# A norm, a projection, a convolution and the rates of a state-space branch moved into the steps of the layers that follow; a causal mask and the first fetches moved too

## The reference

```python
xn = layernorm(x)
x = x + L0_attn(xn) + L0_ffn(xn)          # causal, 16 heads; 8 experts, top 2
xn = layernorm(x)
x = x + L1_attn(xn) + L1_ffn(xn)

def L1_attn(x):                            # the branch
    xn = (x - mu) * rsqrt(var + EPS) * gamma + beta
    xin, z = split(xn @ W_in.T + b_in)     # 256 channels each
    xc = silu(causal_conv1d(xin, conv_w, taps=15) + conv_b)
    dt_low, Bm, Cm = split(xc @ W_x.T)     # 8, 16, 16
    delta = softplus(dt_low @ W_dt.T + b_dt)
    h_t = h_(t-1) * exp(delta_t * A) + delta_t * B_t * xc_t   # 16 states
    y = sum_n(h * C) + xc * D_param
    return x + (y * silu(z)) @ W_out.T + b_out

def L1_ffn(x):                             # the layers
    for i in range(6):
        x = attn_layer(shift_tokens(x), ...) + x   # 16 heads of 64, window 32, rotary, l2norm
        x = ffn_layer(shift_tokens(x), ...) + x    # layer norm, 341 gated units, gelu
    return x
```

## Time and profile before

| | us |
|---|---|
| median of 3 runs | 3053.31 |
| lowest, highest | 3052.78, 3054.47 |
| the profiled execution | 3048.94 |
| its span, first to last instruction | 3047.1 |
| attention of block 0 and opening, to the drain | 1208.9 |
| prologue of the layers, to the first instruction of step 0 | 62.1 |
| the rest, steps and tail | 1776.1 |

### The profile page before, as it was taken

One profiled execution on the slowest core, in us unless ns is written; L12 is line 12 of the kernel. 1 busy time (PEld: TensorE's weight loads), 2 busy tenths in 40 slices (PEclk: granted clock), 3 DMA queues, 4 the chain that ended last, 5 costly groups with the idle time before them and its releaser, 6 DMA issues.

```text
span 3047.1 us, 98549 instructions
## 1 busy us (share of the span) xinstructions
PE 2865.7 (94%) x41200; PEld 1881.2 (62%) x41200; DVE 2261.1 (74%) x3547; ACT 1754.5 (58%) x2617; POOL 1672.8 (55%) x1471
## 2 busy tenths in 40 slices
PE   6999999999999998898999999999999999999996
PEld 5555556555666656465666666666666666666664
DVE  2666565584677776877888888887888878888773
ACT  2544555545666665455666566665666666665553
POOL 0000001100466665476888788887788868887652
PEclk7999999999999999999999999999999999999998
DMA  2000000000011111134334334432433343333222
GB/s 92 1 1 1 1 1 1 1 1 10 15 46 46 45 46 40 46 105 125 89 87 117 85 80 117 92 86 76 111 96 89 80 109 93 80 88 81 68 68 56
DMA packets 181658, 188.24 MB, mean 62 GB/s; under 512 B 77598, under 2 KB 128548, under 8 KB 179684
## 3 DMA queue, kind: packets, MB, share of 16 engines
q1 hardware_dynamic: 181220, 181.94, 23.8%
HBM read 60.99 MB, written 6.03 MB: 22 GB/s over the span
## 4 chain that ended last, share of the span: by engine, by line
PE 78%; DVE 8%; issue 5%; ACT 3%; SPq 3%; POOL 2%; DMA 1%; DVEq 0%; ACTq 0%; POOLq 0%
PE ps L1318 16%; PE ps L581 13%; PE ps L1326 5%; PE ps L1411 5%; PE ps L1369 5%; PE ps L1333 5%; PE ps L616 4%; PE ps L594 4%; PE ps L1378 2%; PE ps L528 2%; PE ps L1432 2%; PE ps L1425 2%; PE ps L599 2%; DVE nmx L685 2%; PE ps L1359 2%
## 5 line engine op out<-in xcount | busy, mean ns | idle before, releaser
L1318 PE MATMUL ps<-wqkv,xcT 128*128 128x512 f32 x1152 | 558.2, 607 | 53.6 <-issue 31.9
L581 PE MATMUL ps<-xnT,qp 128*128 128x512 f32 (+3 forms) x1280 | 527.5, 543 | 15.5 <-ACT prob L803 14.6
L1934 POOL TENSOR_TENSOR ra<-ra,rb 128x1024 f32<-128x1024 f32 x192 | 452.1, 2360 | 160.7 <-DVE rb L1814 159.9
L811 ACT ACTIVATE probT<-ps 128x512 f32<-128x512 f32 (+3 forms) x384 | 207.7, 541 | 385.8 <-PE ps L594 385.8
L803 ACT ACTIVATE prob<-ps,ebias,unit 128x1024 f32<-128x1024 f32 (+7 forms) x384 | 360.3, 954 | 113.8 <-DVE ebias L692 55.0
L581 PEld LDWEIGHTS ps<-xnT,qp 128*128 128x128 f32 x1280 | 232.2, 191 | 272.2 <-issue 227.7
L1953 POOL TENSOR_TENSOR ra<-ra,rn 128x1024 f32<-128x1024 f32 x192 | 361.6, 1904 | 7.5
L1318 PEld LDWEIGHTS ps<-wqkv,xcT 128*128 128x128 f32 x1152 | 196.0, 190 | 222.1 <-issue 208.3
L685 DVE TENSOR_REDUCE nmx<-ps 128x1 f32<-128x1024 f32 (+7 forms) x256 | 245.7, 986 | 109.7 <-PE ps L581 95.3
L1589 ACT ACTIVATE sq<-ps 128x1024 f32<-128x1024 f32 x192 | 195.2, 1017 | 95.8 <-PE ps L1318 95.4
L1812 DVE TENSOR_TENSOR ra<-ps,tab 128x1024 f32<-128x1024 f32 x192 | 233.0, 1213 | 0.0
(11 more groups left out here) (278 smaller groups left out, 5724.0 us busy)
## 6 DMA issues: line engine op xcount, KB each, us to landing
vw<-vs SPq DMA_DIRECT2D x576, 130.0 KB
vw<-vs SPq DMA_DIRECT2D x384, 65.0 KB
bc<-bc_scratch SPq DMA_DIRECT2D x128, 128.0 KB, 3.0
area<-bc_scratch SPq DMA_DIRECT2D x128, 128.0 KB, 4.3
wqkv<-lwqkv_dram SPq DMA_DIRECT2D x6, 1536.0 KB, 8.7
xc<-xs SPq DMA_DIRECT2D x96, 32.0 KB
wo<-lwo_dram SPq DMA_DIRECT2D x6, 512.0 KB, 10.2
area<-ys SPq DMA_DIRECT2D x24, 128.0 KB
```

Of the source, the lines that this page charges most:

```text
L581: mm = E.matmul(ps[:, 2 * r + o // 512, 0:w], k.qp[:, group % 2, g % NTH * P:(g % NTH + 1) * P], k.xnT[:, k0 + o:k0 + o + w], start=True, ...
L1318: mm = E.matmul(to[:, c, :], k.xcT[:, n % 4, :], k.wqkv[l % 2][:, at + 512 * c:at + 512 * (c + 1)], start=True, stop=True)
L1934: G.tensor_tensor(k.ra[:, n % 2, w, :], k.ra[:, n % 2, w, :], k.rb[:, w, :], ALU.add).then_inc(s("added_" + what), 1)
```

## The change

1. **Attention of block 0, rows 0 to 127**: the mask is no longer a matmul on PE; DVE adds it in PSUM to the last 128 columns, ahead of its maximum (`top`). Rows 128 to 255 keep the matmul.
2. **First fetches**: the transposes' source tiles 0 and 1 of the layers are fetched by SP during the attention, once POOL has written the first half of `xs` (a new event, "first").
3. **Prologue**: PE now begins with the two fetched tiles and the projections of tile 0; then come `turn_heads` and `output`, then q and k of tile 1. `turn_hat`, `project_in` and the convolution have left it. POOL makes the rotary table first, clears less, and no longer makes diagonal weights.
4. **Norms**: `norms_dve` is split: `residual_dve` in the prologue, `centre_dve` and `variance_dve` in step 0, `normal_dve` in step 1. The square root and reciprocal are replaced by two powers on POOL at the end of its step 0 (`deviations`). `turn_hat` is in step 1.
5. **Input projection**: `project_in(m)` in steps 2 to 5, one m each (`IN_STEPS`), with its copies or Silu on ACT.
6. **Convolution**: all on DVE, 30 instructions over 1024 columns, four in each of steps 3 to 5 and three in each of steps 6 to 11, two of them ahead of `shift` and the others behind `normalise` (`conv_share`). Its Silu is in step 12, `factors` in step 13, `rates` in 15 and 16.
7. **Scan**: units from step 21, a chunk every 18 steps.
8. **Buffers and SP**: the padded input of the convolution lies where the second layer's weights go, so that these are loaded at step 12 and no longer at 5, behind a wait for the convolution. The arrays of the branch go to DRAM at steps 4, 5, 12, 13 and 16; at 16 SP also waits until they have landed.

```diff
+def fetch_tile(k, n):
+
+    S, s, b, t = k.sy, k.sem, n % 2, n % NT
+    S.dma_start(k.xc[:, b, 0:DH], k.xs[:, t + 1, 0:DH]).then_inc(s(f"xc{b}"), 16)
+    S.dma_start(k.xc[1:P, b, DH:P], k.xs[0:P - 1, t + 1, DH:P]).then_inc(s(f"xc{b}"), 16)
+    S.dma_start(k.xc[0:1, b, DH:P], k.xs[P - 1:P, t, DH:P]).then_inc(s(f"xc{b}"), 16)
...
 def attention_sp(k):
...
+    S.wait_ge(s("half_pool"), k.ev["pool"].at["first"])
+    fetch_tile(k, 0)
+    fetch_tile(k, 1)
...
-        diag = k0 + nk == (g + 1) * P
+        diag = row >= ROWS // 2 and k0 + nk == (g + 1) * P
...
+        if row < ROWS // 2:
+            V.tensor_tensor(of[:, nk - P:nk], of[:, nk - P:nk], k.causal32[:], ALU.add).then_inc(s("v"), k.v.up())
+            V.wait_ge(s("v"), k.v.n)
...
-CONV = [(0, 0, 512), (0, 512, 512), (1, 0, 128)]
-CONV_PE = [(1, 128, 512), (1, 640, 384)]
+CONV = [(0, t) for t in range(3)] + [(a, t + 3 * (1 - a)) for t in range(KC - 3) for a in (1, 0)] + [(1, t) for t in range(KC - 3, KC)]
+CONV_FIRST, CONV_LAST = 3, 11
+IN_STEPS = {2: 0, 3: 1, 4: 2, 5: 3}
+SILU_STEP, FACTOR_STEP, RATE_STEPS = CONV_LAST + 1, CONV_LAST + 2, {CONV_LAST + 4: 0, CONV_LAST + 5: 1}
+
+
+def conv_share(n):
+
+    if not CONV_FIRST <= n <= CONV_LAST:
+        return []
+    at = [0]
+    for i in range(CONV_FIRST, n + 1):
+        at.append(at[-1] + (4 if i < CONV_FIRST + 3 else 3))
+    return list(range(at[-2], at[-1]))
+
+
+def heads_dve(k):
 
...
-    V.wait_ge(s("ln_std"), 2)
-    V.reciprocal(st[:, 2:4, :], st[:, 0:2, :]).then_inc(s("v"), k.v.up())
-    V.wait_ge(s("v"), k.v.n)
+
+
+def normal_dve(k):
+    V, s = k.ve, k.sem
+    xn, st = k.xn[:, NTH:NT, :], k.st[:, :, 0:NTH]
+    V.wait_ge(s("ln_std"), 3)
     V.tensor_tensor(xn, xn, bcast(st[:, 3, :], 2, P), ALU.mult).then_inc(s("ln_done"), 1)
     V.wait_ge(s("ln_done"), 2)
     V.tensor_tensor(k.hat, xn, bcast(st[:, 2, :], 2, P), ALU.mult).then_inc(s("hat"), 1)
-    V.tensor_copy(k.xs[:, NTH + 1:NT + 1, :], xn).then_inc(s("copied"), 1)
-
-
-def conv_dve(k):
+
+
...
+def conv_dve(k, i):
     V, s = k.ve, k.sem
-    V.wait_ge(s("padded"), 1)
-    V.wait_ge(s("small"), 80)
-    for t in range(KC):
-        for i, (a, o, w) in enumerate(CONV):
-            if t == 0:
-                V.wait_ge(s("in_out"), 2 * a + 2)
-                ins = V.tensor_scalar(k.mu[:, a, o:o + w], k.mxp[:, a, o:o + w], k.taps[:, a, 0:1], k.cols[:, 6 + a:7 + a], ALU.mult, ALU.add)
-            else:
-                V.wait_ge(s("v"), k.v.n - 2)
-                ins = V.scalar_tensor_tensor(k.mu[:, a, o:o + w], k.mxp[:, a, o + t:o + t + w], k.taps[:, a, t:t + 1], k.mu[:, a, o:o + w],
-                                             ALU.mult, ALU.add)
-            if t < KC - 1:
-                ins.then_inc(s("v"), k.v.up())
-            else:
-                ins.then_inc(s("conv"), 1)
-                k.v.n += 1
-    k.v.n -= len(CONV)
+    a, t = CONV[i]
+    x, y = k.mxp[:, a, :], k.mu[:, a, :]
+    if t == 0:
+        V.wait_ge(s("padded"), 1)
+        V.wait_ge(s("in_out"), 2 * a + 2)
+        ins = V.tensor_scalar(y, x[:, 0:TH], k.taps[:, a, 0:1], k.cols[:, 6 + a:7 + a], ALU.mult, ALU.add)
+    else:
+        V.wait_ge(s("v"), k.conv_at[a])
+        ins = V.scalar_tensor_tensor(y, x[:, t:t + TH], k.taps[:, a, t:t + 1], y, ALU.mult, ALU.add)
+    if t < KC - 1:
+        ins.then_inc(s("v"), k.v.up())
+        k.conv_at[a] = k.v.n
+    else:
+        ins.then_inc(s("conv"), 1)
...
-FIRST_UNIT = 8
-CHUNK_STEPS = NS + 4
+FIRST_UNIT = 21
+CHUNK_STEPS = NS + 2
...
+        else:
+            S.wait_ge(s("conv"), ET)
...
-        if n % NT == (5 if n < NT else 2) and n // NT + 1 < L:
+        if n % NT == (CONV_LAST + 1 if n < NT else 2) and n // NT + 1 < L:
...
+        if n == 4:
+            save_sum()
+            save_gate(0)
+        if n == 5:
+            S.wait_ge(s("saved"), 16)
+            load_forward(0)
+            save_gate(1)
+        if n == SILU_STEP:
+            save_convolved()
+        if n == FACTOR_STEP:
             save_factors()
-            S.wait_ge(s("saved"), 32)
-        if n == 3:
+        if n == max(RATE_STEPS):
             save_rates()
-        if n == 4:
             S.wait_ge(s("bc_saved"), 64)
-            load_forward(0)
+            S.wait_ge(s("saved"), 48)
     S.wait_ge(s("mo_saved"), 16 * NCH // 2)
     S.wait_ge(s("v_mm"), NT * (L - 1))
...
-    turn_heads()
     side(-3)
-    output()
     side(-2)
     project_q(0)
     project_k(0)
     project("v", 0, ("v_out", 1))
-    side(-1)
-    turn_hat()
-    E.wait_ge(s("small"), 80)
-    for m in range(4):
-        project_in(m)
+    turn_heads()
+    output()
     project_q(1)
     project_k(1)
-    conv()
+    side(-1)
...
-        if n == 0:
-            factors()
-        elif n <= ET:
-            rates(n - 1)
+        if n == 1:
+            turn_hat()
+        if n in IN_STEPS:
+            E.wait_ge(s("small"), 80)
+            project_in(n, IN_STEPS[n])
         if n < NTILE:
             values(n, 1)
         if n + 1 < NTILE:
             turn_rows("q", n + 1)
             turn_rows("k", n + 1)
+        if n == FACTOR_STEP:
+            factors(n)
+        if n in RATE_STEPS:
+            rates(n, RATE_STEPS[n])
...
+        taps = conv_share(n)
+        for i in taps[:2]:
+            conv_dve(k, i)
         if n < NTILE:
             shift(n)
+        if n == 0:
+            centre_dve(k)
         if 1 <= n <= NTILE:
             finish(n - 1)
+        if n == 1:
+            normal_dve(k)
...
+        what, m = forward_step(n)
+        gate_first = n == FACTOR_STEP or n in RATE_STEPS
+        if gate_first:
+            gated(m, int(what[2]))
+        if n == 0:
+            variance_dve(k)
+        for i in taps[2:]:
+            conv_dve(k, i)
...
+    def deviations():
+        G.wait_ge(s("ln_var"), 2)
+        for i in (3, 2):
+            st = k.st[:, i, 0:NTH]
+            G.tensor_tensor(st, st, k.half[:].broadcast_to([P, NTH]), ALU.pow).then_inc(s("ln_std"), 1)
```

231 lines of the change are left out of this document (110 added, 121 removed).

## The result

The changed kernel takes 3061.0 us (median of 12 executions, 3057.8 to 3066.0); the kernel before, on the same chips, 3050.6. The ratio is 1.0033, with a 95% interval of 1.0024 to 1.0042: slower by 10 us, where 3039.4 and a range up to 3059 were forecast. The profiled execution took 3057.8 us, the fastest of the 12; its span is 3056.0, 8.9 more than that of before.

What follows compares the result with a forecast made beforehand. PE, busy for 94% of the span, was taken to bound the kernel. Mask -7.7, prologue -40.5 and steps +34.3 made -13.9 us, so 3053.3 became 3039.4 us, with a range of 3016 to 3059.

Steps and rivals of the forecast that it cites:

- the prediction's line on step 12: Step 12: loads of 2 MB and ACT's table change with two Silus ahead of the q and k copies, +2.3 us.
- things not thought of: Whole kernel: unnamed causes, counted with two slower outcomes in the 0.11 chance of a slower kernel.
- The prologue: Between attention and step 0: work leaves PE and POOL's chain sets the length, -40.5 us, bounds 36 and 45.
- The mask: Attention rows 0 to 127: PE loses 128 mask instructions of 0.06 us in a full stream, -7.7 us.
- Rival (d): First half of attention: the mask on DVE opens PE's stream, +11 instead of -7.7, 3058 us; chance 0.09.
- Step 0 and step 1: `centre_dve` delays a copy, +2.5; DVE and PE wait for POOL's powers, +6.7; `turn_hat` +1.0; clock +1.8 us.
- the taps: Steps 3 to 11: 30 convolution operations on DVE exceed its idle time and meet POOL, +13.9 us.
- (a): Steps 3 to 11: taps meet POOL at random, 21 instead of 7.4 us, 3053 in all; chance 0.13.
- (b): Steps 3 to 11: every tap waits out a POOL scaling or addition, 49 instead of 7.4 us, 3081; chance 0.08.
- the stall of step 5: Step 5: PE's wait for spread values behind two 1 MB stores goes as these move, -5.0 of 6.3 us.
- Rival (c): Taps and SP's wait are hidden in idle time, without 13.9 and 4.3, 3021 us; chance 0.20.
- SP's wait at step 16: Steps 17 and 18: waiting for the last rate and its landing delays tile 21's fetch, +3.5, clock +0.8 us.

Runs made afterwards that it cites:

- e3: The kernel before with only the causal mask of rows 0 to 127 moved from PE to DVE: 3044.7 us, ratio 0.9987.
- e1: The changed kernel with the DMA of layer 1's head lengths put back at SP's step 5: 3041.2 us, ratio 0.9978.
- e5: e1 with POOL's two powers put ahead of `better` and the scaling of tile 2: 3036.7 us, ratio 0.9957.
- e4: e1 with 26 of the 30 taps left out: 3029.1 us, ratio 0.9938.
- e8: e1 with the second tap ahead of `shift` put between the two halves of `normalise`: 3038.9 us, ratio 0.9969.
- e13: e1 with powers first, `centre_dve` behind the probabilities' copy, Silus behind ACT's copies, taps shared out anew, delta's store a step later: 3029.9 us, ratio 0.9928.
- e14: e13 with SP's store of delta and its waits back at the end of step 16: 3029.5 us, ratio 0.9936.
- e15: The kernel before with only the scan moved, units from step 21 and a chunk every 18 steps: 3051.2 us, ratio 1.0000.

## Why the prediction was wrong

**The step that failed** is the prediction's line on step 12, "loads of 2 MB and a change of ACT's table with two long Silus", together with what it left out of the move in part 8 of the change. It counted the weights of `load_layer(1)` and not its third DMA, and it asked who waits on PE for what was loaded, and not whose queue stands at it. POOL's `tables` came up only in the prologue. Step 11 was forecast at 20.5 and took 41.5 us; POOL stood 30.4 us at its table, PE 18.75 behind it. No rival named it; it was in the 0.11 for slower and "things not thought of". With this one DMA in its old place the kernel has 0.9978 x 3050.6 = 3043.9 us against the 3039.4 forecast, and the range would have held it. But the gain is then 6.7 us and not 13.9: the mask gave less, and steps 20 to the end took more.

**The prologue**: right, -40.4 against -40.5; and 40.6 between e3 and e1, which share the mask. PE began step 0 behind `turn_rows`, and that behind POOL's chain with the mask's cast at its end, as was said:

```profile
1220.86 1.03 POOL L2061 CAST band<-qT 128x1024 bf16<-128x1024 f32 x1
1222.00 3.45 PE L1374 MATMUL ps<-ident,ra 128*128 128x128 f32 x16 [3.14 <-issue]
```

That the number fits to 0.1 is luck in part: `turn_rows` began 18.3 us behind the drain where 19.1 had been counted, and took 3.45 us at half clock instead of 2.

**The mask**: mechanism right (21.32 us a head against the 21.4 announced, no wait in the stream), size wrong: -2.9 and not -7.7. Of the -5.2 in the first table 1.6 is not the mask's: the first row of that execution began so much earlier (67.0 against 68.6). The term counted PE's stream and no change in the clock's spells around it. Rival (d) is out.

**Step 0 and step 1**: step 1 was to take 24 us with DVE waiting for POOL's powers. It took 24.7:

```profile
1249.97 3.76 POOL L2002 TENSOR_TENSOR ra<-ra,rn 128x1024 f32<-128x1024 f32 x2
1253.70 3.27 POOL L2027 TENSOR_TENSOR st<-st,half 128x8 f32<-128x8 f32 x2
```

```profile
1257.00 1.23 DVE L1099 TENSOR_TENSOR ys<-ys,st 128x1024 f32<-128x1024 f32 x1 [5.18 <-POOL st L2027]
```

DVE, idle from 1251.8, waits until 1257.0, 11.9 us into the step (12.3 forecast). e5 confirms it by taking it away. The powers took 1.63 each, as in the earlier trace rows.

**Steps 2 to 11**: the taps were priced at 13.9, and e4 measures 12 for 26 of the 30. In the changed kernel all 30 average 1.40 us (1.5 forecast) and the 28 with two inputs in SBUF 1.44, against rivals (a) and (b), which begin at 2.0:

```profile
L1115 DVE SCALAR_TENSOR_TENSOR area<-wqkv,taps,area x28: 1253/1276/3279, 1288.6 to 1454.9; 128x1024 f32<-128x1024 f32 x28
```

The median is that of the undisturbed tap in the earlier trace rows, 1.28; three of the 28 are longer, 2.00, 3.14 and 3.28, and lose 4.6 us where 7.4 had been counted. The taps cost more in step 11 and less in steps 4 and 7 to 9 than was spread over them: only 6.5 of the 10.5 us by which e4 is shorter in steps 3 to 11 lie in steps 3 to 10. So the total was met with parts that were off both ways, which is luck in part. The taps account for most of the 8.5 us by which steps 0 to 10 beat the forecast, and the stall of step 5 for most of the rest. It is gone altogether: 18.8 us with four taps and a projection, 17.7 with the projection alone (e4), 22.6 before, so that more than the 5.0 taken came back. Rival (c), taps hidden, is out.

**The rule weighed**, that a DVE instruction with two SBUF inputs and a GpSimd instruction that reads SBUF exclude each other (the Trainium skill, "SBUF — State Buffer", section "Who interferes with whom"): the traces agree, and e8 shows it at will, 3.17 for 1.28 us. What was wrong was to look for the price on DVE alone. The change's own taps lose 4.6 us by it, and POOL's small operations beside them 12 (e1 against e4). That whoever issues first keeps the other out fits most places; the operation in the last section, which the profile has begin ahead of two taps and end behind both, does not fit it.

**Steps 12 to 19**: +15.4 against 14.1. Step 13 took 23.1, with 3.6 for `factors` and a pause of 1.44 us behind the Silus. SP's wait at step 16 was seen where it was announced, and smaller:

```profile
1592.59 0.33 SPq L1297 DMA_DIRECT2D delta_scratch<-area  x1
1596.93 0.48 SPq L505 DMA_DIRECT2D xc<-xs  x1
```

```profile
1601.20 0.30 PE L1443 MATMUL ps<-ident,xc 128*128 128x128 f32 x1 [0.69 <-DMA xc<-xs]
```

The store is issued 14.4 us into step 17 and lands 4.3 later, where 8.1 was taken from the earlier trace rows, from a store issued 0.64 us behind another of 1 MB (1347.42 and 1348.06 in the trace of before); PE waits 0.69 and not 3.5. e13 against e14 says that the wait as a whole is worth nothing measurable. Steps 17 to 19 took 59.3 us against 54.3 even so. That is near the 4.3 that had been priced, but PE's wait for the tile is 0.7 of it; what the rest is stays open.

**Open** is what steps 20 to 94 (+3.9) and the tail (+2.6) pay. Steps 24 to 94 take 1.0 to 7.4 us more than before in all 13 traces of changed kernels, 3.6 on average, and the tail 2.1 to 3.9 more; e15 rules out the scan's place by itself. None of the runs tells whether it comes with the scan's place and the earlier start together or with something else.

## What to carry to other kernels

When a step of a DMA queue is moved, list every DMA in the function that is called, and for each one every engine that waits for it, with the place of that wait in the engine's own order; a preparation that nobody needs for four steps stops an in-order queue as hard as a needed one. An idle gap of DVE is a place for a tap only if POOL, which the tap excludes, is idle there too, and the price may show on POOL. Single edits of 1 to 5 us could not be told apart here, since untouched steps moved by 2 to 3 us with the clock's spells and the start of the first row by 5.7 from trace to trace; their sum could. What the trace shows of such an edit is whether the wait that it was made for is gone.

## What the runs showed of the hardware

PE paused for 18.75 us (1453.98 to 1472.73), and its granted clock stood at half, 1.2 GHz, for 20.5 us (1457.7 to 1478.2). So 15.0 us of the spell lay in the pause, where they cost nothing, and 5.5 behind it, where sixteen transposes took 3.80 instead of 1.97. Pauses of 2.4 to 7.0 us in steps 0 and 1 went with spells of 3.4 to 10.2 us, whose place and length differed between kernels with the same code there.

Two taps in a row can hold POOL out over both. Timelines of POOL and DVE in e1, step 10:

```profile
1424.13 2.81 POOL L1995 TENSOR_TENSOR rt<-rn,sx 128x32 f32<-128x32 f32 x1 [5.20 <-ACT rn L1625]
```

```profile
1424.36 2.47 DVE L1115 SCALAR_TENSOR_TENSOR area<-wqkv,taps,area 128x1024 f32<-128x1024 f32 x2
```

An operation of 0.25 us on 32 columns ended only at 1426.94, behind both taps (1426.83), though the profile has it begin 0.23 us ahead of them. It is the exception. In the other six places of this trace where POOL's small operation meets the first of two taps, it ends 0.1 us behind that first one and the next operation waits for the second, as in step 4 (the taps are 1312.39 to 1313.67 and 1313.58 to 1314.86):

```profile
1313.17 0.60 POOL L1995 TENSOR_TENSOR rt<-rn,sx 128x32 f32<-128x32 f32 x1 [6.56 <-ACT rn L1625]
1313.86 1.12 POOL L1997 TENSOR_TENSOR rt<-rt,rn 128x32 f32<-128x32 f32 x1
```

```profile
1312.39 2.47 DVE L1115 SCALAR_TENSOR_TENSOR area<-wqkv,taps,area 128x1024 f32<-128x1024 f32 x2
```

The trace of the changed kernel has the same six and one. What makes the one in step 10 differ, no run shows.
